# Planned durations taken from the trace, attention tiles three ahead, and waits that TensorE's order implies left out, in a four-layer graph network kernel

## The reference, cut to what matters

```
x = layernorm(x + normalized_adj @ (x @ w0) + b0)
x = layernorm(x + L1(x))     # attention, 8 heads of 32, masked where adj == 0; projection o; o + layernorm(o)
x = layernorm(x + L2(x))     # 3 gated (GRU) steps:
#   a = adj @ h; z = sigmoid(a.w3 + h.u3); r = sigmoid(a.w4 + h.u3); c = tanh(a.w5 + (r*h).u5); h = (1-z)h + z c
x = layernorm(x + L3(x))     # attention, 8 heads of 32, with (1 - adj) * -1e9 added to the scores; projection
```

## Time and profile before

| what | value |
|---|---|
| median of three runs | 2742.77 us (2742.54 to 2743.79) |
| the profiled execution's own time | 2742.29 us |
| its span, first to last instruction | 2740.2 us |
| mean granted TensorE clock | 0.987 of full speed |
| TensorE records | 2617.4 us (96%), 17448 matmuls |
| TensorE weight loads | 2060.4 us (75%) |
| VectorE, ScalarE, GpSimd busy | 1990.4, 1923.1, 722.0 us |

### The profile page before, as it was taken

One profiled execution on the slowest core, in us unless ns is written; L12 is line 12 of the kernel. 1 busy time (PEld: TensorE's weight loads), 2 busy tenths in 40 slices (PEclk: granted clock), 3 DMA queues, 4 the chain that ended last, 5 costly groups with the idle time before them and its releaser, 6 DMA issues.

```text
span 2740.2 us, 52235 instructions
## 1 busy us (share of the span) xinstructions
PE 2617.4 (96%) x17448; PEld 2060.4 (75%) x17448; DVE 1990.4 (73%) x6107; ACT 1923.1 (70%) x4278; POOL 722.0 (26%) x1065
## 2 busy tenths in 40 slices
PE   4999999999999999999999999999999999999997
PEld 3777777787777878777777777878777787777775
DVE  5767858767687785867778687685867868665776
ACT  3757857768586685868758587685957758674776
POOL 1222331321413222132231413223132321323211
PEclk8999999999999999999999999999999999999999
DMA  3312202122131221302122121221212112021122
GB/s 111 70 24 47 47 26 60 25 62 47 29 67 29 47 47 39 70 17 62 32 52 58 35 52 40 47 47 33 66 28 57 38 45 64 16 47 24 31 49 61
DMA packets 85096, 126.79 MB, mean 46 GB/s; under 512 B 15265, under 2 KB 34145, under 8 KB 84833
## 3 DMA queue, kind: packets, MB, share of 16 engines
q1 hardware_dynamic: 84832, 123.47, 19.0%
HBM read 14.36 MB, written 8.39 MB: 8 GB/s over the span
## 4 chain that ended last, share of the span: by engine, by line
PE 86%; DVE 5%; ACT 4%; issue 3%; POOL 1%; SPq 1%; DMA 0%; DVEq 0%; ACTq 0%; POOLq 0%
PE bank L1174 17%; PE bank L1175 16%; PE bank L1176 16%; PE bank L1233 15%; PE bank L1248 9%; PE bank L1225 7%; ACT probs L741 2%; PE bank L1253 2%; PE bank L1216 1%; PE bank L1286 1%; PE bank L1193 1%; ACT PT L751 1%; DVE PT L993 1%; SPq L568 1%; POOL feat L678 1%
## 5 line engine op out<-in xcount | busy, mean ns | idle before, releaser
L741 ACT ACTIVATE probs<-probs,few 128x512 f32<-128x512 f32 x1024 | 731.1, 717 | 83.9 <-DVE few L981 78.9
L981 DVE CUSTOM_DVE_ANT_0 probs<-bank,mask 128x512 f32<-128x512 f32 x1024 | 682.5, 687 | 82.9 <-issue 63.1
L1233 PE MATMUL bank<-ident,probs 128*128 128x128 f32 x4096 | 608.9, 275 | 31.6 <-ACT probs L741 24.9
L1233 PEld LDWEIGHTS bank<-ident,probs 128*128 128x128 f32 x4096 | 484.3, 141 | 142.2 <-issue 47.1
L751 ACT ACTIVATE PT<-bank 128x512 f32<-128x512 f32 x634 | 368.3, 594 | 116.6 <-PE bank L1233 56.2
L1225 PE MATMUL bank<-stack 96*128 96x512 f32 x1024 | 443.0, 457 | 0.7 <-DVE few L981 0.4
L993 DVE COPY PT<-bank 128x512 f32<-128x512 f32 x390 | 265.3, 687 | 85.1 <-PE bank L1233 61.0
L1248 PE MATMUL bank<-PT,vh 128*32 128x256 f32 x4096 | 260.7, 386 | 12.2 <-DVE PT L993 4.5
L1174 PE MATMUL bank<-feat,W 128*128 128x512 f32 x640 | 261.9, 409 | 2.6 <-POOL feat L678 2.2
L661 POOL TENSOR_TENSOR feat<-o,feat 128x256 fp32r<-128x256 f32 x128 | 94.9, 741 | 610.3 <-ACT feat L764 610.1
L1176 PE MATMUL bank<-feat,W 128*128 128x512 f32 x640 | 252.8, 395 | 0.0
(11 more groups left out here) (117 smaller groups left out, 5081.5 us busy)
## 6 DMA issues: line engine op xcount, KB each, us to landing
stack<-qk SPq DMA_DIRECT2D x768, 128.0 KB, 2.4
res<-in_x_dram SPq DMA_DIRECT2D x16, 512.0 KB, 3.8
out_dram<-res SPq DMA_DIRECT2D x16, 512.0 KB, 2.9
PT<-in_adj_dram SPq DMA_DIRECT2D x1, 1024.0 KB, 5.4
PT<-in_L_gnn_w_w_dram SPq DMA_DIRECT2D x2, 512.0 KB, 6.7
raw<-in_L_gnn_w_qkv_dram SPq DMA_DIRECT2D x1, 768.0 KB, 9.7
vh<-in_L_gnn_w_w_dram SPq DMA_DIRECT2D x1, 512.0 KB, 8.0
res<-in_L_gnn_u_w_dram SPq DMA_DIRECT2D x2, 256.0 KB, 7.9
```

Source lines behind the costliest of these rows:

```text
L741: k = act.activation(p, p, ACT.Exp, bias=least[:, t % P_RING:t % P_RING + 1], scale=-1.0, accum_out=sums[:, grp % 2, q * HG + h:q * HG + h ...
L981: k = dve.tensor_tensor_reduce(out=probs[:, t % P_RING, :], in0=place("scores", t)[:, :], in1=mask[:, half * QT + q, :], scale=1.0, scalar ...
L1233: k = pe.transpose(place("transpose", t)[:, m * P:(m + 1) * P], probs[:, t % P_RING, m * P:(m + 1) * P], ident[:, :])
```

## The change

1. `AHEAD` is 3 in place of 2: in the plan, scores wait for the `stt` three tiles back, and transposes for the `pt` three tiles back.
2. Durations and delays are no longer arguments of `add`. `nominal` looks them up by the kind of piece. A `pt` has one duration on ScalarE and another on VectorE, and where both could start it at the same time, the shorter wins. Delays go from 0.1 us for nearly all pieces to 0.11 to 0.28 us by kind.
3. VectorE's `stt` and both `move_pt` leave out the wait for transposes or `values` where TensorE's list has these before the piece whose result is waited for anyway. The memset in front of an `stt` stays only where the piece before it on VectorE is an `stt` too.

No arithmetic and no instruction of TensorE, ScalarE, GpSimd or SyncE is added or removed but for waits.

```diff
-AHEAD = 2
+AHEAD = 3
...
+TILE_US = {"scores": 0.31, "stt": 0.61, "exp": 0.71, "transpose": 0.36, "recip": 0.12, "rsum": 0.62}
+PT_US = {"ACT": 0.48, "DVE": 0.61}
+VALUES_US = {1: (1.86,), 2: (0.89, 1.19)}
+PE_US = {"ax": 2.8, "a": 2.8, "proj1": 1.93, "proj3": 1.93, "hT": 0.36, "x1T": 0.36, "x2T": 0.36, "x3T": 0.36}
+ACT_US = {"scale": 0.4, "n0": 0.99, "n1": 0.99, "n2": 0.99, "n3": 0.99, "rows2": 0.95, "q": 0.55, "k": 0.55, "r": 0.61,
+          "zt": 0.61, "c": 0.61, "rh": 0.52, "hf": 0.52, "out0": 0.26, "out2": 0.31}
+DVE_US = {"scale": 0.4, "w0": 1.66, "mom_o": 0.93, "norm_o": 2.52, "rows2": 1.14, "h": 2.06, "res2": 1.55, "proj3": 1.55,
+          "out1": 0.34}
+POOL_US = {"scale": 2.35, "beta": 2.35, "out3": 0.7}
+SP_US = {"load": 0.6, "store": 0.6, "stack": 1.9}
+
+LATE = {"scores": 0.13, "stt": 0.11, "exp": 0.25, "transpose": 0.28, "pt": 0.25, "recip": 0.2, "rsum": 0.2, "values": 0.25,
+        "pe": 0.2, "act": 0.14, "dve": 0.2, "pool": 0.15, "load": 3.5, "store": 3.0, "stack": 2.4}
...
+def nominal(key):
+    kind, what = key[:2]
+    if kind in TILE_US:
+        us = TILE_US[kind]
+    elif kind == "pt":
+        us = PT_US
+    elif kind == "values":
+        us = VALUES_US[PARTS][key[2]]
+    elif kind == "pe":
+        us = PE_US.get(what, 1.4)
+    elif kind == "act":
+        us = ACT_US.get(what, 0.48)
+    elif kind == "dve":
+        us = DVE_US.get(what, 0.61)
...
+    return us, LATE[kind]
...
+def took(piece, engine=None):
+    return piece.us if not isinstance(piece.us, dict) else piece.us[engine] if engine else max(piece.us.values())
...
-                    rank = (start, -way[piece.key])
+                    rank = (start, -way[piece.key], took(piece, e))
...
-        add("scores", "PE", 0.235, ("scores", t), ("stack", layer, b, g, h),
+        add("scores", "PE", ("scores", t), ("stack", layer, b, g, h),
             *([("stt", t - AHEAD)] if t >= AHEAD else []), opens=[("scores", t)])
-        add("stt", "DVE", 0.68, ("stt", t), ("scores", t), *([("transpose", t - P_RING)] if t >= P_RING else []),
+        add("stt", "DVE", ("stt", t), ("scores", t), *([("transpose", t - P_RING)] if t >= P_RING else []),
             frees=[("scores", t)])
-        add("exp", "ACT", 0.72, ("exp", t), ("stt", t), *([("rsum", grp - 2)] if grp >= 2 else []))
-        add("transpose", "PE", 0.44, ("transpose", t), ("exp", t), *([("pt", t - AHEAD)] if t >= AHEAD else []), opens=[("transpose", t)])
-        add("pt", ("ACT", "DVE"), 0.56, ("pt", t), ("transpose", t),
+        add("exp", "ACT", ("exp", t), ("stt", t), *([("rsum", grp - 2)] if grp >= 2 else []))
+        add("transpose", "PE", ("transpose", t), ("exp", t), *([("pt", t - AHEAD)] if t >= AHEAD else []), opens=[("transpose", t)])
+        add("pt", ("ACT", "DVE"), ("pt", t), ("transpose", t),
...
-                add("values", "PE", 1.7 / PARTS + 0.2, ("values", grp, part), *(() if part else tail),
+                add("values", "PE", ("values", grp, part), *(() if part else tail),
...
-                        add(dve, "DVE", 2.3, ("dve", "h", b, s, o), ("act", "c", b, s, o), ("act", "zt", b, s, o))
+                        add(dve, "DVE", ("dve", "h", b, s, o), ("act", "c", b, s, o), ("act", "zt", b, s, o))
...
+        place_on_pe = {key: i for i, key in enumerate(order.by_engine["PE"])}
+        before_on_dve = dict(zip(order.by_engine["DVE"][1:], order.by_engine["DVE"]))
+
+        def pe_has_passed(key, by):
+
+            return place_on_pe[key] < place_on_pe[by]
...
-                if t >= P_RING:
-
+                if t >= P_RING and not pe_has_passed(("transpose", t - P_RING), by=("scores", t)):
                     wait_full(dve, "transpose", t - P_RING)
-                apart()
+                if before_on_dve["stt", t][0] == "stt":
+                    apart()
...
-                if t >= PT_RING:
-
+                if t >= PT_RING and not pe_has_passed(("values", (t - PT_RING) // GROUP, PARTS - 1), by=("transpose", t)):
                     wait_full(dve, "values", (t - PT_RING) // GROUP)
```

More of the change, by code:

```diff
@@ L43, in raised_by @@
         self.next += 1
+TILE_US = {"scores": 0.31, "stt": 0.61, "exp": 0.71, "transpose": 0.36, "recip": 0.12, "rsum": 0.62}
[24 more added lines that the diff above has]
+        us = DVE_US.get(what, 0.61)
+    elif kind == "pool":
+        us = POOL_US.get(what, 1.24) if what != "rstd" else 1.0 if key[3] == "no" else 1.65
+    else:
+        us = SP_US[kind]
+    return us, LATE[kind]
 Piece = namedtuple("Piece", "key engines us late after opens frees")
+def took(piece, engine=None):
+    return piece.us if not isinstance(piece.us, dict) else piece.us[engine] if engine else max(piece.us.values())
 class Order:
@@ L56, in __init__, with add @@
         self.queues, self.by_engine, self.banks = {}, {}, {}
-    def add(self, queue, engines, us, key, *after, late=0.1, opens=(), frees=()):
+    def add(self, queue, engines, key, *after, opens=(), frees=()):
         engines = (engines,) if isinstance(engines, str) else engines
+        us, late = nominal(key)
         self.queues.setdefault(queue, []).append(Piece(key, engines, us, late, after, opens, frees))
@@ L78, in ways @@
         for key in reversed(line):
-            way[key] = pieces[key].us + pieces[key].late + max([way[k] for k in then.get(key, ())], default=0.0)
+            way[key] = took(pieces[key]) + pieces[key].late + max([way[k] for k in then.get(key, ())], default=0.0)
         return way
@@ L110, in run @@
             left -= 1
-            clock[e] = start + piece.us
+            clock[e] = start + took(piece, e)
             done[piece.key] = clock[e] + piece.late
@@ L165, in adj_resnorm_kernel, with evacuated @@
     add = order.add
[L167 to L172, removed]
+    def evacuated(b, name, f):
+        add(("act", b % STREAMS), "ACT", ("act",) + name + (f,), ("pe",) + name + (f,))
+        add(("dve", b % STREAMS), "DVE", ("dve",) + name + (f,), ("act",) + name + (f,), frees=[name + (f,)])
     for b in bs:
@@ L194, in adj_resnorm_kernel @@
         for tp in range(NT // 2):
-            add(act, "ACT", 0.75, ("act", "n0", b, tp), ("pool", "rstd", b, "n0", tp))
+            add(act, "ACT", ("act", "n0", b, tp), ("pool", "rstd", b, "n0", tp))
         for layer in (1, 3):
@@ L233, in adj_resnorm_kernel @@
                     for o in range(FT):
[L234 to L237, removed]
+                        add(pe, "PE", ("pe", "z", b, s, o), ("dve", "a", b, s, FT - 1))
@@ L249, in adj_resnorm_kernel @@
                     for o in range(FT):
[L250 to L252 removed]
+                        add(pe, "PE", ("pe", "c", b, s, o), ("pool", "rh", b, s, FT - 1))
+                        add(act, "ACT", ("act", "c", b, s, o), ("pe", "c", b, s, o), frees=[("c", b, s, o)])
@@ L265, in adj_resnorm_kernel @@
                 for tp in range(NT // 2):
-                    add(act, "ACT", 0.75, ("act", "n2", b, tp), ("pool", "rstd", b, "n2", tp))
+                    add(act, "ACT", ("act", "n2", b, tp), ("pool", "rstd", b, "n2", tp))
             xT, last = (("x1T", b), "n0") if layer == 1 else (("x3T", b), "n2")
             for f in range(FT):
-                add(pe, "PE", 0.5, ("pe",) + xT + (f,), ("act", last, b, 1), opens=[xT + (f,)])
+                add(pe, "PE", ("pe",) + xT + (f,), ("act", last, b, 1), opens=[xT + (f,)])
@@ L278, in adj_resnorm_kernel @@
                 first = (block_at[layer, b] * TILES + g * HALVES * GROUP)
                 for h in range(HG):
-                    add(sp, "SP", 1.9, ("stack", layer, b, g, h), ("dve", "k", b, layer, g),
-                        *([("stt", last_of_head(first, h))] if first else []), late=2.4)
+                    add(sp, "SP", ("stack", layer, b, g, h), ("dve", "k", b, layer, g),
+                        *([("stt", last_of_head(first, h))] if first else []))
             for tp in range(NT // 2):
-                add(pe, "PE", 6 * MM, ("pe", "v", b, layer, tp), opens=[("v", b, layer, tp)])
@@ L292, in adj_resnorm_kernel @@
         for tp in range(NT // 2):
-            add(act, "ACT", 0.75, ("act", "n3", b, tp), ("pool", "rstd", b, "n3", tp))
-        add(sp, "SP", 0.5, ("store", b), ("act", "n3", b, 1), late=3.0)
+            add(act, "ACT", ("act", "n3", b, tp), ("pool", "rstd", b, "n3", tp))
+        add(sp, "SP", ("store", b), ("act", "n3", b, 1))
     for t in range(len(BLOCKS) * TILES):
```

92 lines of the change are left out of this document (48 added, 44 removed).

## The result

The changed kernel takes 2657.91 us (2656.05 to 2658.42, four runs) against 2743.05 us before: a ratio of 0.9688, 95% interval 0.9671 to 0.9705, 3.1% faster. The forecast was 2711 us with a range down to 2672, so the sign was right, the size 85 us in place of 32, and the time lies under the range. The profiled execution has a span of 2656.5 us and took 2658.25 us.

What follows compares the result with a forecast made beforehand. TensorE's work plus the moments it stands was taken to bound the kernel; 28 us from tile stops, 4 from stream stops and 0 from dropped waits took 2742.8 us to 2711 us, likeliest range 2690 to 2733, whole range 2672 to 2762.

Steps and rivals of the forecast that it cites:

- The room: TensorE's standing time that the change could win, over the whole span: about 99 us, 3.6% of the span.
- a stop is shown too short by about 0.2 us: TensorE's records outlive their slots, so some 100 stops behind the preparation hide some 20 us more.
- the forecast's own check: In the changed profile, TensorE's busy time stays within 10 us of 2617; its idle total is 85 to 100 us.
- Half of the tile stops: TensorE's stops in the attention tiles, 55 us with the hidden share: 28 us of them come back.
- if ScalarE were filled wholly, ... 51% of these stops: Three longest tiles-only stretches, 64 us: a full ScalarE saves 6.9 us against 10.6 us idle TensorE plus some 3 hidden.
- Streams: TensorE's stops in the stream work, 35 us with the hidden part: 4 us gained, as a list can only be lucky.
- Clock: Long TensorE stops drop the clock to half rate; some 4 us at half clock costs 1.6 us more per place.
- Part 3: Waits and memsets left out on VectorE: gain taken as 0, at most 1 us passed on.
- The reason given for the two parts together: Third tile ahead and nominal times give a better order, not less work; they act on 55 us of tile stops.
- Rival (a): More than half comes back: all 55 us of tile stops and 10 of the stream stops, 2678 us; chance 0.15.
- Rival (c): Slower: tile chain runs dry more often, 6.2 us per place; eight more places give 2761 us; chance 0.17.
- The Trainium skill's rule on bubbles and room in PSUM: A repeating TensorE bubble can mean no room for the next tile; third tile ahead cures all 55 us: 2688 us.

## Why the prediction was wrong in size

**The room was read too small.** The step "a stop is shown too short by about 0.2 us", times some 100 listed stops, made 20 us of hidden time and 99 us of room. The records shrank by 40.6 us, and the forecast's own check (TensorE's busy time within 10 us of 2617) failed. The idle time outside the records, forecast at 85 to 100 us, came to 79.7. Where this lies is seen from the starts of the matmuls. I took each from its start to the next start, less the median of the same pair of matmuls at full clock with no idle time between; what is left over is an estimate of the time lost. Behind the first 42 us, in us:

| where the time is lost | before | after |
|---|---|---|
| idle outside the records | 75.2 | 32.2 |
| part of such a stop that the record before it covers | 24.7 | 10.4 |
| stops that a record covers wholly, so that no wait is listed | 38.0 | 27.2 |
| matmuls at the lower clock | 19.3 | 5.7 |

The second line is the 20 us of the prediction, rightly sized. The third and the fourth were put at nothing, though together they held 57 us of room; they gave 11 and 14 us; the second line gave 14. A busy time counts overlapping records once, and a sum over listed stops can't see the third line; most of it (27.8 and 21.3 us) lies between the first and the second pass of a product.

The groups of the profile do not show where records shrank, tempting as they are. The transposes and scores of the changed kernel:

```profile
L1279 PE MATMUL bank<-ident,probs 128*128 128x128 f32 x4096 | 588.6, 273 | 11.0 <-ACT probs L789 8.6 <-ACT PT L798 0.5 <-DVE PT L1039 0.4
L1271 PE MATMUL bank<-stack 96*128 96x512 f32 x1024 | 422.3, 453 | 0.7 <-DMA stack<-qk 0.5
```

Before, the same two were

```profile
L1233 PE MATMUL bank<-ident,probs 128*128 128x128 f32 x4096 | 608.9, 275 | 31.6 <-ACT probs L741 24.9 <-DVE few L981 3.8
L1225 PE MATMUL bank<-stack 96*128 96x512 f32 x1024 | 443.0, 457 | 0.7 <-DVE few L981 0.4
```

The fall of 20.3 + 20.7 = 41 us looks like all of the 40.6. But all groups together fell by 65 us, since records of different groups overlap. Scores followed directly by scores stand 153 times in the order before and 258 times after, and two such records overlap: 0.94 us for three in the timeline above, 0.48 for one alone. That lowers the busy time of the group and wins nothing by itself.

**Half of the tile stops was too little.** The step that failed is "if ScalarE were filled wholly, ... 51% of these stops". In the listed stops 40.4 us became 12.5, 69% gone. The limit took VectorE's and ScalarE's 88 and 89% in the long stretches as work that must be done there. The stretches at 768 to 2262 above have TensorE at 100% with ScalarE at 87 to 100%. The long ones no longer occur, and stretches of 4 us or more lose 14.5 us in place of 43.7, all together. My reading, which no run shows by itself, is that in the mixed parts before them the tiles had been carried farther. A bound from the busy share of a stretch holds only while the order keeps the stretch as it is, and here the order was the change. Only the last one, with nothing to mix in, still shows the limit (TensorE 84%, ScalarE 93%).

**Streams.** I took 4 of 35 us and called the rest a matter of luck. The listed part fell from 29.9 to 17.6, so 12 us and the hidden share of ten stops more. The places of the earlier trace rows are gone. I had priced each at 6.2 us; by the starts of the matmuls they cost 7.3, 8.0 and 7.5 us, stops and clock together. I had used that price only for the rival that they get more. Nor were they three: the trace before has two more long drops of the clock behind 700 us, at 2487 and 2651, and in the changed kernel two short ones are left (3.4 us each, near 2277 and 2407). And the level in rows 6 fell at 708.5 us, after the first long stop, not after all of the 8 us before 712.

**Clock.** I counted it in the price of a long stop and as nothing in the gain. It gave some 14 us, as worked out above, partly the same as in the last point.

**Part 3** was right: taken at 0, bounded by 1 us, measured 1.2 us on the old order (the interval of the ratio includes no change) and 1.1 us on the new.

**The reason given for the two parts together** (a better order, not less work) held, but I had no term for what they do to each other. Alone the third place gave 35 us, about what I forecast for both, and the new numbers 11; 38 us more came only together. Rival (a), more than half comes back, named the mechanism and priced it at 2678 us with a chance of 0.15; the result lies 20 us beyond it. Rival (c), more dry places, did not happen with three ahead, nor with four (1332 behind `vh`: 0.2 us in both). The stops behind `h` came back in another run, with the transposes alone three ahead:

```profile
PE bank L1332 <- DVE vh L1129: 17.9, 10, 3.6
```

The Trainium skill's rule on bubbles and room in PSUM (Perfetto Trace Analysis, Identifying Performance Opportunities), by which I let all 55 us of the tile stops go, came nearer in time (2688 against my 2711). For the stops themselves it did not: of the listed ones 69% went. And it isn't the whole cure: the third place in the plan without right delays gave 2736.2 us, and a fourth lost 62.

Why the parts multiply can be read from the planner in good part. Each kernel's static lists, timed again with the new table (durations, delays, banks in their order, no `AHEAD` terms), come to 2630.5 us before, 2622.5 with new numbers alone, 2589.5 with three ahead alone and 2551.7 with both. That is an estimate without the preparation; the measured times lie 106 to 117 us above it. By it the parts give 8 and 41 us and both 79, where 11, 35 and 84 were measured. So most of what comes only with both is in the lists and the table already, and such a count, made before the run, would have forecast 79 us in place of 32. It also shows the loss with four ahead (2598). For new durations with old delays it gives 2605 us, where that plan's own table says 2559. What stays open is the rest, up to some 25 us between these runs, and which piece of an order does it.

## What to carry to other kernels

Where a static order is made from a cost table, the table's delays between engines count as much as its durations: measure both from start to start in the trace, set both together, and rather too late than too early. Try the depth of the lookahead again after each such correction, one step at a time, since its best value is sharp (2731, 2658 and 2720 us for two, three and four here). Size the room of such a change from start-to-start times of the bounding engine, not from its list of waits, and time the new lists with the measured table before the run.

## What the runs showed that I had not expected

Half of the time that was won (40.6 of 83.7 us) was never listed as idle: it lay under the overlapping records of short matmuls and in matmuls at the lower clock. And small shifts in a greedy planner's numbers, by 0.01 and 0.02 us in the new table or by 0.1 us in the old one, move this kernel by 11 and 8 us, more than many of the edits that one would want to measure; the repeat with an unchanged list came out the same (2657.9 and 2657.8).
